# Attention's loop over the batches, written out on every engine of a fused FFN, attention, FFN block

## The reference, cut to what matters

```python
x = x + 0.5 * ffn(layernorm(x), w_gate, w_up, w_down)   # inner width 704, inputs and weights rounded to FP4 blocks of 16
z = layernorm(x)
Q, K, V = z @ Wq, z @ Wk, z @ Wv
scores = Q @ K.T / sqrt(256); scores above the diagonal = -inf
x = x + softmax(scores) @ V
x = x + 0.5 * ffn(layernorm(x), w_gate, w_up, w_down)
```

## Time and profile before

| what | value |
|---|---|
| median of three runs | 1251.25 us (1249.59 to 1252.75) |
| profiled execution | 1254.0 us, span of its instructions 1252.2 us |
| mean granted TensorE clock, share of full speed | 0.986 |
| TensorE matmul busy | 1159.9 us, 93% of the span |
| VectorE busy | 1005.8 us, 80% |
| ScalarE busy | 791.5 us, 63% |
| GpSimd busy | 554.8 us, 44% |
| DMA, share of 16 engines | 53.1% (queue 1, the transposes) |
| instruction packets, queue 8 | 42, 0.69 MB |
| instruction packets, queue 14 | 38, 0.31 MB |

### The profile page before, as it was taken

One profiled execution on the slowest core, in us unless ns is written; L12 is line 12 of the kernel. 1 busy time (PEld: TensorE's weight loads), 2 busy tenths in 40 slices (PEclk: granted clock), 3 DMA queues, 4 the chain that ended last, 5 costly groups with the idle time before them and its releaser, 6 DMA issues.

```text
span 1252.2 us, 24913 instructions
## 1 busy us (share of the span) xinstructions
PE 1159.9 (93%) x7673; PEld 751.6 (60%) x7673; DVE 1005.8 (80%) x2809; ACT 791.5 (63%) x1599; POOL 554.8 (44%) x531
## 2 busy tenths in 40 slices
PE   1789999999997699989998999999999999999996
PEld 1356666666655456756675667566656666666664
DVE  6899999999999566456545654664689999999995
ACT  4768888888855254434543553566578888888852
POOL 2444555444544145424542444445344445455541
PEclk9889999999999899999999999999999999999999
DMA  6955444444444367646663666547245555555575
GB/s 214 239 102 87 93 93 86 93 94 94 91 79 90 71 116 110 117 89 100 115 120 78 114 101 117 103 77 135 40 90 120 119 119 111 111 116 112 112 120 108
DMA packets 462752, 134.48 MB, mean 107 GB/s; under 512 B 441296, under 2 KB 461904, under 8 KB 462672
## 3 DMA queue, kind: packets, MB, share of 16 engines
q1 hardware_dynamic: 454928, 125.62, 53.1%
q10 hardware_dynamic: 7744, 7.86, 2.0%
HBM read 11.34 MB, written 8.39 MB: 16 GB/s over the span
## 4 chain that ended last, share of the span: by engine, by line
PE 74%; DVE 13%; issue 5%; ACT 3%; DMA 2%; POOL 1%; SPq 1%; DVEq 0%; ACTq 0%; POOLq 0%
PE ps L1481 32%; PE ps L1442 17%; PE ps L1528 12%; PE ps L1516 9%; PE ps L1501 2%; PE ps L1494 2%; DVE arena L1138 2%; DMA arena<-arena 2%; ACT arena L797 1%; DVE arena L969 1%; DVE arena L973 1%; DVE arena L1030 1%; SPq L418 1%; ACT arena L789 1%; DVE arena L1101 1%
## 5 line engine op out<-in xcount | busy, mean ns | idle before, releaser
L1481 PE MATMUL ps<-wguT,arena 128*128 128x512 f16 (+1 forms) x2304 | 480.9, 363 | 5.7 <-DMA arena<-arena 5.7
L1481 PEld LDWEIGHTS ps<-wguT,arena 128*128 128x128 f16 x2304 | 226.1, 98 | 227.8 <-issue 11.2
L549 POOL TENSOR_TENSOR arena<-arena 128x704 f32<-128x704 f32 x128 | 193.8, 1514 | 252.6 <-DVE arena L982 252.6
L1442 PE MATMUL ps<-wdT,arena 128*128 128x256 f16 x2176 | 263.6, 276 | 25.8 <-DMA arena<-arena 17.6
L1442 PEld LDWEIGHTS ps<-wdT,arena 128*128 128x128 f16 x2176 | 214.5, 99 | 68.6 <-DMA arena<-arena 16.2
L576 POOL TENSOR_TENSOR arena<-arena 128x128 f16<-128x128 f32 (+7 forms) x64 | 143.9, 2249 | 239.3 <-ACT arena L797 199.9
L806 ACT ACTIVATE arena<-ps,arena,cst 128x128 f16<-128x128 f32 (+7 forms) x64 | 80.5, 1258 | 196.4 <-DVE arena L1143 189.7
L1528 PE MATMUL ps<-arena 128*128 128x256 f16 x1632 | 188.8, 273 | 12.2 <-DVE x_sb L1154 11.8
L1516 PE MATMUL ps<-arena 128*128 128x512 f16 (+3 forms) x960 | 188.9, 349 | 3.5 <-ACT arena L797 3.5
L1528 PEld LDWEIGHTS ps<-arena 128*128 128x128 f16 x1632 | 158.0, 98 | 40.5 <-DVE x_sb L1154 11.0
L720 ACT ACTIVATE arena<-ps,cst 128x704 f32<-128x704 f32 x128 | 108.4, 847 | 77.4 <-PE ps L1481 69.6
(11 more groups left out here) (128 smaller groups left out, 1403.6 us busy)
## 6 DMA issues: line engine op xcount, KB each, us to landing
out_dram<-x_sb SPq DMA_DIRECT2D x32, 256.0 KB, 2.7
x_sb<-in_L_attn_x_dram ACTq DMA_DIRECT2D x3, 2048.0 KB, 9.0
arena<-arena SPq DMA_TRANSPOSE x384, 3.5
arena<-arena SPq DMA_DIRECT2D x8, 256.0 KB, 3.3
arena<-arena SPq DMA_DIRECT2D x4, 512.0 KB, 3.4
x_sb<-in_L_attn_x_dram ACTq DMA_DIRECT2D x1, 1536.0 KB, 7.3
arena<-in_L_ffn_w_down_dram SPq DMA_DIRECT2D x1, 704.0 KB, 8.7
arena<-in_L_ffn_w_gate_dram SPq DMA_DIRECT2D x1, 640.0 KB, 4.5
```

The lines of the kernel that those rows point to most:

```text
L549: g.tensor_tensor(hy[u].rearrange("p (j b) -> p b j", j=BL), h[u].rearrange("p (b j) -> p b j", j=BL), hri[u].unsqueeze(2).to_broadcast([P ...
L1442: i = nc.tensor.matmul(ps_dn[w % 2], hT[w][:, c * P:(c + 1) * P], wdT[:, k, :], start=(s == 0), stop=(s == len(DOWN_STEPS) - 1))
L1481: i = nc.tensor.matmul(psf[:, 1536 * u + lo:1536 * u + hi], xv[:, u, xl, kt, :], wguT[:, wl, lo // P:hi // P, kt, :], start=(s == 0), stop ...
```

## The change

On each of the four engines the hardware loop over batches 0 to 2 is replaced by a Python loop. The body is issued three times with `b` = 0, 1, 2 as a constant. The slots, their order inside the body, the buffers and the semaphores stay. What depended on `b` through a register (a semaphore value, an address in `x_sb`) becomes a constant. The lists grow: built, TensorE's holds 4586 matmuls instead of 3002, and VectorE's 1985 instructions instead of 1644.

```diff
@@ GpSimd @@
                     for s in range(FIRST):
                         pool_slot(0, s)
-                    with pool.Fori(0, B - 1) as b:
+                    for b in range(B - 1):
                         for s in range(FIRST, END):
                             pool_slot(b, s)
@@ def act_attention(act) @@
-            with act.Fori(0, B - 1) as b:
+            for b in range(B - 1):
                 for s in range(FIRST, END):
                     act_slot(b, s)
@@ def dve_attention(dve) @@
-            with dve.Fori(0, B - 1) as b:
+            for b in range(B - 1):
                 for s in range(FIRST, END):
                     dve_slot(b, s)
@@ def pe_attention(pe) @@
-            with pe.Fori(0, B - 1) as b:
+            for b in range(B - 1):
                 for s in range(FIRST, END):
                     pe_slot(b, s)
```

## The result

In six runs each the kernel after takes 1241.55 us (median; 1241.01 to 1242.67) and the kernel before 1249.51 us (1248.82 to 1252.75). The medians are 8.0 us apart. The ratio on record, estimated from all the runs, is 0.9927, 95% interval 0.9915 to 0.9939; of 1249.51 us that is 9.1 us, between 7.6 and 10.6. A second measurement on another occasion gave 1240.51 against 1250.21 us, ratio 0.9925 (0.9911 to 0.9938). Predicted were 1242.5 us and 8.8 us of gain, counted from a median of 1251.25 us for the kernel before.

A forecast was written before the change was run, and what follows sets the result against it. Attention was taken as bound by TensorE's matmuls plus 26.3 us of idle gaps. The two turns' gains, 8.8 us, with all other terms at 0, took the median from 1251.25 to 1242.5 us, range 1239 to 1247 (8 in 10).

The forecast's parts named there:

- The turns: Attention, 48-matmul to 18-matmul group at both loop turns: stretches shrink to 34.22 us, gaining 4.01 and 4.79, in sum 8.80 us.
- The wait ahead of the 18-matmul group: Sign in attention at both former turns: TensorE's wait before slot 8's matmuls would be 0.9 us.
- The cause: At attention's branch back, TensorE and VectorE stall on fetching the large body's instructions; the stall leaves with the branch.
- The first rival: At attention's turns only VectorE's stall leaves and TensorE's pause stays: gain about 4.0 us, 1247.2 us; chance 0.07.
- Does the gain carry through: From the 18-matmul to the next 48-matmul group, still 78.5 us, and through the second FFN: shifts arrive at the end.
- Register instructions: Removed from the loop body: gain already in the turns' sum; batch 0 between nothing and 0.6 us, taken as 0.0.
- The entry: Entry into attention's loop: removing the unconditional branch gains between 0 and 3.4 us, taken as 0.
- Streaming three bodies: Straight code in attention's batches: costs nothing, or up to one 4.45 us stall per batch; taken as nothing.
- Slower, by the FFN loops' place: Rival: second FFN's shifted loops no longer stay on chip, VectorE pays 22.3 us over 5 turns, 1264.8 us; chance 0.04.
- The sum: Whole kernel: median 1251.25 us less 8.8 us gives 1242.45, say 1242.5 us.

The follow-up runs named there:

- the loops that never turn: Kernel after with each written-out batch body inside a hardware loop that runs once, on all four engines: 1243.85 us, ratio 0.9939.
- the moved loop: Kernel after with TensorE's batch loop put back and 96 more instructions ahead of it: 1242.56 us, ratio 0.9928.
- the body of 12 pairs: Kernel after with TensorE's loop in both FFNs made of 2 passes over 12 pairs of tiles instead of 12 over 2: 1243.12 us, ratio 0.9926.

## Why the prediction was right, step by step

**The turns** (predicted 4.01 + 4.79): 38.23 - 34.22 = 4.01 and 39.01 - 34.21 = 4.80 us. The method held: the trace of before contained the passage with and without the jump, and only the missing statistics had to be added. The wait ahead of the 18-matmul group came out at 0.70 us instead of 0.9, and the stretch was right all the same. The group ahead of it shows why; in the last batch of before and at the former first turn of after it stands at:

```profile
805.14 3.09 PE L1516 MATMUL ps<-arena 128*128 128x512 f16 x18
```

```profile
569.42 3.09 PE L1516 MATMUL ps<-arena 128*128 128x512 f16 x18
```

From its start to the 18 matmuls are 808.06 - 805.14 = 2.92 us without a wait and 573.21 - 569.42 = 3.79 us with it: a delay of 0.87 us, as predicted (0.86), of which the profile calls 0.70 idle, because neighbouring groups overlap. So the 0.88 of idle at the second turn did not confirm the 0.86: there the delay was 696.14 - 692.18 - 2.92 = 1.04 us. With ScalarE and GpSimd looped the idle is 0.88 us and the stretch 34.4 us, so the difference is probably theirs.

**The cause** (large body fetched again): right in direction. That the pause needs a jump back is shown by the loops that never turn; that a jump back alone does not make it, by the moved loop; that each engine does it alone, by the loops put back one by one; that it is the code and its place, by the same loop moved by 96 and by 256 instructions, for TensorE. For VectorE the pause was shown with three large bodies (341, 367 and 545 instructions as built) and not with the one of 189, which has register instructions and a branch back too. Whether its place matters was not tried; that its pause is a fetch is read from the packets of queue 14.

**The first rival** (only VectorE's stall leaves, 1247.2): false; TensorE's pause is its own. But the figure behind it, that a body of this size has room in TensorE's memory, was not wrong. It has 1646 instructions and not 1584, since waits and register work count too, and it does have room, from another start.

**Does the gain carry through** (yes): yes, and more. **Register instructions** (taken as 0.0 outside the turns' stretches): this term was mis-sized. From the 18-matmul to the next 48-matmul group it takes 538.99 - 460.92 = 78.07, 651.28 - 573.21 = 78.07 and 763.57 - 685.49 = 78.08 us, against 78.54 and 78.56 and 540.36 - 461.80 = 78.56 in batch 0: 0.48 us a batch, 1.4 us in all. The forecast of 78.5 for this stretch was a miss. The prediction took the two equal times of before for a sign that nothing was there to win; both held small waits for L1154 (in batch 1 0.49 and 0.15 us, against 0.33 and none after). With TensorE alone looped the stretch is 538.97 - 460.83 = 78.14 us; with VectorE alone looped it is 656.92 - 578.45 = 78.47. There is no turn in it, so it is the register work of the looped body, VectorE's mostly. Batch 0's first slots, up to the 18-matmul group, give 0.6 us more (40.75 us before, 40.16 after), which the prediction had named as its upper bound and set to 0.0. Here no engine alone explains it: looped alone, TensorE leaves 40.18, VectorE 40.28, ScalarE with GpSimd 40.30 us.

**The entry** (0): right; the wait for the transpose is 3.5 us, as before. **Streaming three bodies** (0): right, no wait without a releaser is left on TensorE. **Slower, by the FFN loops' place**: it did not happen, but TensorE shows that the place can decide: with the body of 12 pairs the second FFN paid 1.79 us at its turn and the first nothing. The bodies as they are paused at no turn at either place.

**The sum**: 8.8 from the turns and 2.0 from registers make 10.8 us in the profiled pair, against 9.1 us (7.6 to 10.6) in the runs. If the registers give 2.0 us in the runs as well, the turns give about 7 there (9.1 - 2.0; by the medians 6). The turns' price is not constant: VectorE's pause was 4.45 us in the kernel before and 3.12 and 2.72 with VectorE alone looped, and the clock halved behind one of TensorE's pauses and not behind the other. Whether the profiled turns of before lay high by chance, or two engines that fetch side by side slow each other, was not measured apart. So the total is in part luck: the sum left out 2.0 us and had the turns about 2 us too dear for an ordinary execution, and the two errors pull opposite ways. The time has a little luck of the same kind: the median of before was 1.7 us lower in the six runs than in the three that the forecast started from, and the gain of the medians 0.8 us smaller than forecast, which leaves the time 0.9 us under the forecast.

## What to carry to other kernels

Look at each engine's branch back in the chain of waits: a pause with no releaser between two marks of the sequencer at the loop's line, and instruction packets beside it, were the signs here that the body is fetched again. Two engines that pause side by side hide each other: with one of the two still looped, about 7 of the 9 us stayed lost. Writing the loop out cures it; on TensorE moving the loop by 96 instructions did the same for its pause, and an edit ahead of a large loop can undo it, as the move by 256 did.

## What the runs showed of the hardware that I had not expected

A loop of 1646 instructions on TensorE turned without any pause when it stood 96 instructions further on, and paused 2.3 to 2.8 us a turn at its old place and 256 further on. When it pauses, the whole body is read again (17 more packets for two turns). The packets bring 16 KB on queue 8 (42, 0.69 MB, in the kernel before) and 8 KB on queue 14 (38, 0.31 MB). A wait that is long satisfied is not free: 512 of them, in 256 instructions, put TensorE's first matmul 17.5 us later (30.56 us) than in the run with 192 (13.08 us), whose 96 instructions hid in the 13 us that it waits there anyway.
